# A gated input taken on chip, a reordered opening and a last result in halves

## What is computed

```python
xn = _layernorm(x)
x = x + attn(xn, ...) + ffn(xn, ...)

# attn: linear attention block on xn
x = x + dwconv(x, cpe1)                      # 3 taps along the tokens
xn = ln(x); act_res = silu(xn @ actp_w + actp_b)
xi = silu(dwconv(xn @ in_w + in_b))
q, k = elu(xi @ qk_w + qk_b) + 1; ...        # rope, k^T v per head, times q, times z
x = shortcut + (attn + dwconv(xi, lepe)) * act_res @ out_w + out_b
x = x + dwconv(x, cpe2); x = x + gelu(ln(x) @ fc1_w + fc1_b) @ fc2_w + fc2_b

# ffn: gated network with ternary weights and a scale per output
h = silu((xn @ w1.T) * w1_s) * ((xn @ w2.T) * w2_s)
h = gelu((h @ h1.T) * h1_s); h = gelu((h @ h2.T) * h2_s)
return (h @ w3.T) * w3_s
```

## Time and profile before

| what | value |
|---|---|
| median of 3 runs | 1075.15 us (1072.56 to 1079.33) |
| the profiled execution | 1074.53 us |
| its span, first to last instruction | 1072.7 us |
| mean granted clock of TensorE over the span | 0.993 |
| PE, PEld busy | 96%, 85% |
| DVE, ACT, POOL busy | 71%, 56%, 22% |
| moved by DMA | 180.68 MB, 168 GB/s on the mean |

### The profile page before, as it was taken

One profiled execution on the slowest core, in us unless ns is written; L12 is line 12 of the kernel. 1 busy time (PEld: TensorE's weight loads), 2 busy tenths in 40 slices (PEclk: granted clock), 3 DMA queues, 4 the chain that ended last, 5 costly groups with the idle time before them and its releaser, 6 DMA issues. The chain is left out here.

```text
span 1072.7 us, 17199 instructions
## 1 busy us (share of the span) xinstructions
PE 1027.1 (96%) x6644; PEld 910.2 (85%) x6644; DVE 759.4 (71%) x956; ACT 603.7 (56%) x874; POOL 238.4 (22%) x214
## 2 busy tenths in 40 slices
PE   3899999999999999999999999999999999999997
PEld 3678877888877777877788889999899999999997
DVE  6884689534548568988887657867787968776664
ACT  4678667676444364655655535555655654655444
POOL 3444255224305021111001031222200211101100
PEclk9999999999998999999999999999999999999999
DMA  8978615966784635423322473243494423222210
GB/s 303 422 238 338 219 52 178 331 209 206 261 289 142 198 126 207 160 97 109 127 79 79 156 295 117 86 134 118 148 367 174 157 79 119 90 77 87 103 40 22
DMA packets 68402, 180.68 MB, mean 168 GB/s; under 512 B 5040, under 2 KB 26160, under 8 KB 64688
## 3 DMA queue, kind: packets, MB, share of 16 engines
q1 hardware_dynamic: 68320, 179.56, 48.1%
HBM read 121.86 MB, written 66.06 MB: 175 GB/s over the span
## 5 line engine op out<-in xcount | busy, mean ns | idle before, releaser
L2226 PE MATMUL pr<-xp_hi,wb 128*128 128x256 f32 x1344 | 320.0, 282 | 0.9 <-DVE u L1978 0.7
L2226 PE MATMUL pr<-xp_lo,wb 128*128 128x256 f32 x1344 | 319.5, 281 | 0.0
L2226 PEld LDWEIGHTS pr<-xp_hi,wb 128*128 128x128 f32 x1344 | 255.3, 190 | 2.7 <-issue 2.7
L2226 PEld LDWEIGHTS pr<-xp_lo,wb 128*128 128x128 f32 x1344 | 255.8, 190 | 0.0
L2226 PE MATMUL pr<-u_hi,ring 128*128 128x512 f32 x256 | 102.5, 400 | 1.8 <-POOL u_lo L931 1.0
L2226 PE MATMUL pr<-u_lo,ring 128*128 128x512 f32 x256 | 100.0, 391 | 0.0
L1416 ACT CAST xp_hi<-tf 128x1024 fp32r<-128x1024 f32 x48 | 50.2, 1046 | 56.4 <-PE pr L2226 19.9
L1050 POOL TENSOR_TENSOR ot<-ot,yg 128x512 f32<-128x512 f32 x14 | 25.2, 1802 | 244.3 <-DVE ot L2009 244.3
L1831 DVE TENSOR_TENSOR h_lo<-hf,h_hi 128x512 fp32r<-128x512 f32 x64 | 54.6, 862 | 32.6 <-ACT h_hi L1356 32.6
L2411 PE MATMUL pr<-wf_hi,h_hi 128*128 128x256 f32 x256 | 75.3, 294 | 0.6 <-DVE h_lo L1831 0.6
L1972 DVE TENSOR_TENSOR xp_lo<-tf,xp_hi 128x1024 fp32r<-128x1024 f32 x48 | 60.8, 1266 | 20.2 <-ACT xp_hi L1416 20.1
(11 more groups left out here) (230 smaller groups left out, 2526.7 us busy)
## 6 DMA issues: line engine op xcount, KB each, us to landing
ring<-w_s SPq DMA_DIRECT2D x42, 512.0 KB, 7.4
uf<-h_s SPq DMA_DIRECT2D x16, 1024.0 KB, 5.1
wb<-s_s SPq DMA_DIRECT2D x8, 1024.0 KB, 9.2
wb<-w_s SPq DMA_DIRECT2D x6, 1024.0 KB, 9.9
vw<-v_s SPq DMA_DIRECT2D x8, 514.0 KB, 6.8
xt<-x SPq DMA_DIRECT2D x8, 512.0 KB, 6.0
xn_s<-xh SPq DMA_DIRECT2D x8, 512.0 KB, 9.6
stage<-w_gated SPq DMA_DIRECT2D x2, 2048.0 KB, 13.5
```

The costliest lines, as they stand in the source:

```text
L2226: return e.matmul(bank, w.bitcast(dt), v_.bitcast(dt), start=first, stop=last, skip_group_check=True)
```

## The change

SP issues tile 0 of x ahead of the parameters and no longer loads the first gated input from DRAM. ACT splits it from `xh[0]`, where `copy_xn(0)` has put it, and `copy_xn(2)`, which overwrites `xh[0]`, waits until POOL has made the low part from it too. DVE's program no longer starts with the wait for the parameters. The orders on DVE, ACT and POOL in the opening change as the diff shows. For the last result of the last tile, DVE, ACT and PE work in two halves of [128, 2, 256] with a semaphore step for each; the number of matmuls is the same, 16.

```diff
@@ sync @@
+            load_x(0)
             sp.dma_start(prm[:], t["params"]).then_inc(s["prm_in"], 16)
-            load_x(0)
...
-            load_xg(0, xg1)
             save_xn(1)
             fill_ring()
@@ gpsimd @@
             halo(1, xh, "xh_w", 1, "xh_halo")
+            low_of_xg(0, xg1_lo, mid(xh[0]), xg1_hi)
+            inverse_deviation(0, "b", "b_applied")
             inverse_deviation(2, "a", "a_applied")
-            inverse_deviation(0, "b", "b_applied")
             inverse_deviation(3, "a", "a_applied")
             halo(2, xh, "xh_w", 1, "xh_halo")
-            low_of_xg(0, xg1_lo, xg1, xg1_hi)
@@ scalar @@
+                if i == 2:
+                    e.wait_ge(s["x_split"], 1)
                 e.copy(mid(xh[i % 2]), X[:]).then_inc(s["xh_w"], 1)
...
             def high_of_xg(j, x_hi, xf):
-                e.wait_ge(s["xg_in"], 16 * (j + 1))
+                if j > 0:
+                    e.wait_ge(s["xg_in"], 16 * j)
...
             split_attn_weights()
+            high_of_xg(0, xg1_hi, mid(xh[0]))
             conv1_centre(1)
+            apply_norm(0)
             apply_xn(2)
-            apply_norm(0)
-            apply_xn(3)
             high_of_norm(0)
             copy_xn(2)
-            high_of_xg(0, xg1_hi, xg1)
+            apply_xn(3)
             xi_out(0)
...
+            def last_result(h):
+                t_, before = BLOCK_RUNS + TILES - 1, len(RESULTS) * (TILES - 1)
+                e.wait_ge(s["u_sum"], 5 * t_ + 5 + h)
+                for m in range(2 * h, 2 * h + 2):
+                    last = e.activation(results[3][:, m, :], u2[:, m, :], ACT.Gelu,
+                                        scale=par("h2_s", RESULTS[3][0] * HB + m))
+                last.then_inc(s["c_gelu"], 1)
+                e.wait_ge(s["c_gelu"], gelus(t_, 3) + 2 * h)
+                e.wait_ge(s["down_mm"], before + 1)
+                e.copy(a_hi[3][:, 2 * h:2 * h + 2, :], results[3][:, 2 * h:2 * h + 2, :]).then_inc(s["c_gelu"], 1)
@@ vector @@
-            e.wait_ge(s["prm_in"], 32)
...
             xn_moments(0)
+            apply_xn(0)
             xn_moments(1)
-            apply_xn(0)
             apply_xn(1)
+            e.wait_ge(s["prm_in"], 32)
+            conv1_side(0, False)
             check_staged(range(0, 1))
-            conv1_side(0, False)
             conv1_side(0, True)
...
-            check_staged(range(1, 2))
             low_of_attn_weights()
-            check_staged(range(2, FIRST_LAYER))
+            check_staged(range(1, 3))
             low_of_norm(0)
+            check_staged(range(3, FIRST_LAYER))
+            staged_bits(0, FIRST_LAYER)
             conv1_side(1, False)
-            staged_bits(0, FIRST_LAYER)
             conv1_side(1, True)
...
+            def last_result_21(h):
+                t_, part = BLOCK_RUNS + TILES - 1, slice(2 * h, 2 * h + 2)
+                e.wait_ge(s["prod"], NP * t_ + 7)
+                e.wait_ge(s["u_sum"], 5 * t_ + 4)
+                e.tensor_tensor(u2[:, part, :], quarters(pr[1])[:, part, :], u2[:, part, :], ALU.add) \
+                    .then_inc(s["u_sum"], 1)
+
+            def low_of_last_result(h):
+                part = slice(2 * h, 2 * h + 2)
+                e.wait_ge(s["c_gelu"], gelus(BLOCK_RUNS + TILES - 1, 3) + 1 + 2 * h)
+                e.tensor_tensor(a_lo[3][:, part, :], results[3][:, part, :], a_hi[3][:, part, :].bitcast(F32), ALU.subtract) \
+                    .then_inc(s["a_lo"], 1)
@@ tensor @@
+            def last_down(wide):
+                half, tokens = RESULTS[3]
+                for c in range(HB):
+                    e.wait_ge(s["a_lo"], len(RESULTS) * (TILES - 1) + 4 + c // 2)
+                    for i in range(2):
+                        for n, v_ in enumerate((a_hi[3], a_lo[3])):
+                            last = add(as_tokens(down_banks)[:, 2 * tokens + i, :], v_[:, c, i * P:(i + 1) * P],
+                                       wd[:, half * HB + c, :], wide, False, c == HB - 1 and n == 1)
+                last.then_inc(s["down_mm"], 1)
```

More of the change, by code:

```diff
@@ L1495, in _ @@
                 for k, ps in ((1, ()), (2, (4, 5)), (3, (6,))):
-                    gelu_block(t_, k)
-                    high_of_result(r, k)
+                    if k == 3 and not more:
+                        for h in range(2):
+                            last_result(h)
+                    else:
+                        gelu_block(t_, k)
+                        high_of_result(r, k)
                     if more:
@@ L2100, in _ @@
                 low_of_result(r, 2)
-                result_21(t_)
                 if more:
+                    result_21(t_)
                     low_part(t_ + 1, 4)
                     low_part(t_ + 1, 5)
-                low_of_result(r, 3)
-                if more:
+                    low_of_result(r, 3)
                     low_part(t_ + 1, 6)
+                else:
+                    for h in range(2):
+                        last_result_21(h)
+                    for h in range(2):
+                        low_of_last_result(h)
             e.wait_ge(s["y_in"], 16 * TILES)
@@ L2500, in product @@
                 last.then_inc(s["prod"], 1)
+            def last_down(wide):
[7 more added lines that the diff above has]
+                last.then_inc(s["down_mm"], 1)
             def down(r, k, wide):
                 half, tokens = RESULTS[k]
+                if r == TILES - 1 and k == 3:
+                    last_down(wide)
+                    return
                 e.wait_ge(s["a_lo"], len(RESULTS) * r + k + 1)
```

## The result

| kernel | median us | runs | ratio to before, 95% interval |
|---|---|---|---|
| before, as shown ahead | 1075.15 | 3 | |
| before, beside the change | 1074.77 | 5 | 1 |
| after | 1067.28 (1065.33 to 1069.73) | 5 | 0.9934 [0.991, 0.9958] |
| after, on another chip (f2 below) | 1068.15 | 11 | 0.9952 [0.9933, 0.9971] |

Two executions fell in a slow state, one of f2 (1252.70 us) and one of f1 (5681.74 us); every median here leaves them out.

The account below looks back on a forecast made before the run. PE, busy 96% of the span, was taken to bound the kernel, its loss at both ends. Opening 0.9 plus end 1.45 us made 2.35 us: 1072.8 us from a median of 1075.15, range 1069.2 to 1076.6 us.

Parts of the forecast that it names:

- Reading of the profile: Whole program: only PE's 45 us without a matmul can be won, lost at both ends; ACT's apply_xn(3) holds the opening's chain.
- Part 1: Opening, x loaded first and DVE not waiting for the parameters: transposes of the convolved tile at 18.94 us, gain 0.3 us.
- Part 2: Opening, gated input taken on chip: ACT's copy hidden, POOL's low_of_xg 2.40 us beside statistics; 0.2 us of 0.3 left.
- Part 3: Opening, orders on ACT and POOL: apply_xn(2) from 28.95 us, first large matmul at 33.3 us, 0.95 us earlier (bounds 0.5 to 3.2).
- What is late next: After the first matmuls, norm_tokens(1) on PE: its side taps are done at 38.5 us, PE arrives at 40.55, covered by 2 us.
- Part 4: Program's end, last result in halves: PE runs on without waiting for a_lo, gain 1.45 us (bounds 0 to 1.5).
- The sum: Whole program: 0.9 us for the opening plus 1.45 us for the end, 2.35 us; forecast 1072.8 us, chance 0.60.
- (a): Rival, opening: less PE idling ahead of the first large matmuls keeps the clock up, 1.25 us more, 1071.5 us; chance 0.14.
- (b): Rival: opening's gain lost on the way to a wait that doesn't shift, only the end won, 1073.7 us; 0.18 with (d).
- (c): Rival, in_proj(0) and act_proj(0): clock stays down longer, 18 more slow matmuls, +3.6 us, 1076.4 us; chance 0.08.
- (d): Rival, POOL's order: low_of_xg 1.6 us slower beside DVE, first matmul stays near 34.2 us, 1073.7 us; 0.18 with (b).

Follow-up runs that it names:

- f2: The changed kernel, unchanged, run again on another chip beside the kernel before: 1068.15 us, ratio 0.9952.
- f1: Kernel before with three parts alone: apply_xn(3) behind copy_xn(2), x first with its DVE order, last result in halves: 1068.41 us, 0.9957.
- c3: Changed kernel with ACT's apply_xn(3) again ahead of high_of_norm(0): 1071.82 us, ratio 0.9974 to before.
- d1: Kernel before with one line moved on ACT, apply_xn(3) behind copy_xn(2): 1069.68 us, ratio 0.9967.
- d2: Kernel before with x ahead of the parameters and the DVE order that goes with it, nothing else: 1073.96 us, ratio 0.9992.
- c2: Changed kernel with the first gated input loaded from DRAM again and split at its old places: 1069.22 us, ratio 0.9949 to before.
- c1: Changed kernel with DVE's check 1 again ahead of the weights' low parts, checks 2 and 3 ahead of low_of_norm(0): 1068.92 us, 0.9961 to before.
- b3: Changed kernel with the opening alone, the last result whole again: 1069.38 us, ratio 0.9957 to before.
- e3: Kernel before with the first x issued only once parameters and identity are there: 1075.99 us, ratio 1.0022.
- d3: Changed kernel with its start put off, x and all else loaded only after parameters and identity are there: 1070.85 us, 0.9964 to before.
- d4: Changed kernel with apply_xn(2) ahead of apply_norm(0), POOL's low_of_xg after both deviations, check 2 behind low_of_norm(0): 1070.72 us, 0.9964 to before.
- c5: Changed kernel with the 32 one-column matmuls of offsets_of_mlp split into four groups of 8 between other products: 1071.59 us, 0.9972 to before.

## Why the prediction was wrong

**Reading of the profile: right.** PE's idle time at the two ends was what could be won, and the bystander `apply_xn` on ACT was the piece that held the chain. c3 and d1 show it from both sides.

**Part 1 (0.3 us): right.** The second transposes came at 13.82 and `norm_tokens(0)` at 18.85 us, 0.4 us earlier. The gain of 1.74 us at PE's first transposes was lost to the wait for tile 1, as worked out (a row of 2.52 us on `xt`). d2 has 0.2 us.

**Part 2 (0.2 us left, input on chip hidden): right.** `low_of_xg` had 2.17 us (2.40 taken), `apply_norm(0)` came 0.4 us earlier. That statistics don't disturb it held; c2 shows the part worth nothing at the first matmul. By medians c2 is 1.9 us behind after, but the two intervals overlap widely.

**Part 3 (0.95 us): wrong, and this is the step that failed.** The mechanism was right (the bystander waits for POOL's four operations), the size was not: the term "the fourth is through when the DVE stream stops, about 28.9 us" measured 27.01 us. The step took the trace of before, in which all four operations of tile 3 run beside a DVE stream, 24.85 to 29.87 us, at 1.1 to 1.4 us each. The two in the middle, with DVE beside them:

```profile
25.87 1.41 DVE L1561 SCALAR_TENSOR_TENSOR wq_lo<-wa_raw,prm,wq_hi 128x512 fp32r<-128x512 f32 x2
26.09 1.39 POOL L891 TENSOR_TENSOR rs_a<-rs_a,small 128x4 f32<-128x4 f32 x1
...
27.27 2.54 DVE L1573 SCALAR_TENSOR_TENSOR acc<-stage,acc 128x1024 int32<-128x1024 int32 x2
27.46 1.10 POOL L894 TENSOR_SCALAR nb_h<-mv_a 128x4 f32<-128x4 f32 x1
```

It laid the four of tile 2 into the same stretch, at one DVE instruction each. But they are ready to go as soon as POOL is, and that was 24.00 us, not 24.5: `low_of_xg` started 0.1 us earlier and was 0.23 us shorter, and the two operations behind it took 1.25 us, not 1.4. DVE's stream began at 24.34 us. So the first operation was issued 0.34 us ahead of it (0.20 us), the second 0.06 us ahead of a weight instruction that did not hold it (1.02 us), and the other two had to wait for the rest of a DVE instruction only (0.56 and 1.09 us). The lower bound (26.6 us, by which the first matmul was 31.0) was in the text; the middle was put beside the wrong end. c1 shows what hangs on the order: with the check in place of the weight instruction behind the power operation, 1.1 to 1.3 us are lost again.

**"What is late next": right.** `norm_tokens(1)` came at 38.75 us, 2.74 us earlier than before, so all but 0.1 us of the gain passed it.

**Part 4 (1.45 us): right.** 1.34 us ahead of the last 16 matmuls and 0.1 us within them; no wait for `a_lo`.

**The sum and the medians.** With 2.75 in place of 0.9 us the sum is 4.2 us. The four and four spans differ by 5.8 us in the mean (1071.9 and 1066.1). Of the other 1.6 us, some 0.8 lie in the shorter low stretch near 340 us (1.7 us at half speed), some 0.4 in the slow matmuls of the opening (3.9 us of them before in the mean, 3.1 after), none in `qa`; the last store landed 0.3 us sooner in the profile of after than in that of before. The prediction had no term for these. In the pair of profiles of before and after they looked like 3.3 us won, 1.6 of it at `qa`; repeats of both kernels showed it to be mostly the draw of one execution each. The measured gain is 7.5, 8.0 and 5.3 us by medians. By the ratios it is 7.1 us (4.5 to 9.7) in the first two and 5.2 us (3.1 to 7.2) in the third, so 4.2 us lie inside the third interval and just outside the others. Besides, the median of before that the forecast started from was 0.4 to 1.7 us above those of the five batches.

So the failed step explains only a third of the miss. The median came 5.5 us below the forecast: 1.85 us are part 3, 0.4 us the median that it started from, and about 1.6 us the terms above that the sum didn't have. The last 1.7 us are not explained; against f2's median (4.65 us below) nothing is left. With part 3 at its measured size the forecast would have been 1070.95 us, still above the 1067.28 us. That the change stayed under 1% is no merit of the sum, as every case of the prediction did. Whether the opening itself lowers the share of low clock is open: by the ratios b3 gained 4.6 us (2.9 to 6.2) for 2.6 in the timeline, d1 3.5 us (1.8 to 5.4) for 3.1, and f1 4.6 us (3.0 to 6.3) for 3.2 and the end's 1.4.

**The rivals.** (a), the clock up earlier, did not come in any of four profiles of the changed kernel: its matmuls stay at 0.63 us until 33.4 to 35.6 us. It came in d1 and in d4. The prediction's argument against it, that the bursts of transposes before did not lift the clock, looked at the bursts of 19.25 and 41.49 us only; those of 26.84 to 30.42 us did lift it (last section). In the changed kernel the bystander parts these two bursts by 0.76 us. (b), the opening's gain lost on the way, fell: c3 and d1 carry it to the end, and e3 and d3 show the same of a loss. (c), the clock down longer, fell too. (d) did not happen, and d4 shows what it costs where it does.

## What to carry to other kernels

When small operations of one engine are moved, ask which of them come ahead of the next stream of the other engine and which behind its start, and carry both cases with their own prices: here two operations issued 0.34 and 0.06 us ahead of the stream decided over 1.9 us. An instruction that nobody needs soon, ahead of one that the chain needs, is the first thing to look for in an in-order queue; one moved line did nearly all that the opening's many moves did. And a difference between two profiles at a place which the change doesn't touch should be seen in a second profile of each kernel before it gets a cause.

## What the runs showed of the hardware

Small operations of POOL and DVE can hold each other, and being issued first doesn't protect them: 0.13 us became 1.93 us for DVE in d4, 1.02 became 2.15 us for POOL in c1, where POOL's operation was issued 0.06 us ahead of the check. It isn't so each time: issued 0.06 us ahead of a weight instruction the same operation took 1.02 us.

Transposes can raise TensorE's clock, and don't do so each time. In d1 and d4 the first large matmuls, which follow two bursts of eight transposes each (16 in 3.7 us in d1) and an idle stretch of 0.7 to 0.9 us, take 0.39 to 0.40 us from the second on; in f1 the same order leaves them at 0.63 us until 35.85 us. Over all twenty profiles: where the two bursts stand back to back, the clock was up within 0.6 us of their end in seven of ten; where the second comes 0.76 us or more after the first, in none of ten. This is against the rule of the Trainium skill (TensorE: Matmul & The Clock Gate, Part 4: PE-mode transpose) that a transpose doesn't count as PE work for the clock: there is no large matmul before them in the program, only 16 of one column. The traces don't show whether these transposes run in the mode that the page speaks of.

The kernel before had that rise as well, and lost it. Its clock went up at 30.2 us and fell at 33.6 us, while PE was idle behind the bystander, 0.6 us ahead of the first large matmul:

```profile
32.00:34.00 2.00, 0.00 (x0) 0.00 (x0) 1.09 (x1) 1.78 (x2) 0.16 (x2) 0.90 1.02 413
34.00:36.00 2.00, 1.77 (x4) 1.49 (x5) 2.00 (x4) 1.05 (x1) 0.24 (x3) 0.50 1.06 425
```

The granted clock in the profile doesn't show the whole of it. In the profile of after PEclk stands at 1.00 in this stretch, while its matmuls take 0.63 us until 34.1 us:

```profile
32.00:34.00 2.00, 2.00 (x6) 1.60 (x5) 1.97 (x3) 2.00 (x5) 0.31 (x2) 1.00 1.06 424
```

The first clock entry in that trace is a rise at 34.4 us, where the matmuls turn fast, and PEclk reads 1.00 for all that lies ahead of it. So before the first rise the duration of a matmul is the surer sign, and after's mean clock of 0.997 leaves its slow matmuls out, while before's 0.993 has them in.

Matmuls of one column are busy time to the profile, and the clock fell beside them. PE has no idle time from 326 to 350 us in the profile of before, and 10.2 us of it were granted 0.50. In the nineteen profiles other than c5's the clock fell 1.2 to 4.5 us after the first of these 32. That they are the cause is not shown, as c5 left PE idle there.
